# A convolution block with a cubic spline behind it: two products move from VectorE to GpSimd, one add from TensorE to VectorE

## The reference

```python
# layer 0: sign-weight convolutions, batch norm over the whole batch
out = relu(batchnorm(conv3x3(x, sign(w1)), gamma1, beta1))
x = relu(batchnorm(conv3x3(out, sign(w2)), gamma2, beta2) + x)
# layer 1: a cubic B-spline per channel, 32 control values a = mix @ alpha_table
u = (clip(x * a + b, -1.5, 1.5) + 1) * 0.5 * 31
i, t = floor(u), u - floor(u)
spline = sum over n of alpha_table[clip(i - 1 + n)] * basis_n(t)
return id_gain * x + einsum(spline, mix) + bias
```

## Time and profile before

| what | value |
|---|---|
| median of 3 runs | 1145.0 us (1142.17 to 1150.26) |
| the profiled execution, its own time | 1146.37 us |
| its span, first to last instruction | 1144.5 us |
| TensorE busy | 1082.0 us (95%) |
| VectorE busy | 966.5 us (84%) |
| ScalarE busy | 899.1 us (79%) |
| GpSimd busy | 139.3 us (12%) |
| spline part, first sum to end | 418 to 1144.5 us |

### The profile page before, as it was taken

The page is one execution under the profiler, slowest core; times in us unless marked ns, Lnnn a source line. Parts: engine busy times, 40 slices in busy tenths (PEclk is TensorE's granted clock), DMA queues, the critical chain, the costliest instruction groups (busy, mean ns, idle before and its releaser), DMA issues.

```text
span 1144.5 us, 53175 instructions
## 1 busy us (share of the span) xinstructions
PE 1082.0 (95%) x24650; PEld 733.9 (64%) x24650; DVE 966.5 (84%) x959; ACT 899.1 (79%) x410; POOL 139.3 (12%) x195
## 2 busy tenths in 40 slices
PE   6999999699999968999999999999999999999996
PEld 5777777577777745556676565566666566665564
DVE  4855656696767779999999989989999999999997
ACT  4445443666777648999999999989999999999971
POOL 6000000058100000111101101110101101101000
PEclk9999999899999989999999999999999999999998
DMA  8577674677777837799999989989999998999652
GB/s 275 204 291 281 267 281 170 234 243 289 272 273 298 343 167 159 187 234 225 222 222 227 231 200 228 224 207 233 222 223 217 230 233 196 235 220 226 162 133 87
DMA packets 57465, 259.46 MB, mean 227 GB/s; under 512 B 16080, under 2 KB 16080, under 8 KB 49232
## 3 DMA queue, kind: packets, MB, share of 16 engines
q1 hardware_dynamic: 48496, 208.40, 56.5%
q0 software_dynamic: 8640, 48.17, 22.9%
q10 hardware_dynamic: 160, 0.30, 0.1%
HBM read 104.29 MB, written 77.07 MB: 158 GB/s over the span
## 4 chain that ended last, share of the span: by engine, by line
PE 86%; DVE 7%; issue 4%; DMA 1%; ACT 1%; SPq 0%; DVEq 0%; ACTq 0%
PE tab L1302 48%; PE acc L741 30%; PE tab L1312 7%; DVE middle_mask L1160 1%; DMA halo<-y_scratch 1%; DVE far_sq L1209 1%; DMA w_raw<-in_w 1%; ACT xin L381 1%; ACT yout L420 1%; DVE poly L1201 0%; DVE far L1187 0%; DVE stats L547 0%; DVE offset L1153 0%; DVE poly L1215 0%; DVE band_split L509 0%
## 5 line engine op out<-in xcount | busy, mean ns | idle before, releaser
L1302 PE MATMUL tab<-edge_mask,diag 128*32 128x392 bf16 x10240 | 448.1, 329 | 7.5 <-issue 3.9
L1302 PEld LDWEIGHTS tab<-edge_mask,diag 128*32 128x32 f16 x10240 | 287.4, 97 | 159.4 <-issue 20.5
L1057 ACT ACTIVATE edge_mask<-cell,thr 128x6272 bf16<-128x6272 bf16 x62 | 338.6, 5508 | 1.3 <-DMA cell<-cell 1.3
L420 ACT ACTIVATE yout<-acc 128x1568 f32<-128x1568 f32 x64 | 94.5, 1477 | 169.7 <-PE acc L741 149.1
L741 PE MATMUL acc<-split,w 64*64 64x385 f16 (+3 forms) x4608 | 192.6, 327 | 12.4 <-DVE w L468 10.0
L741 PE MATMUL acc<-band_split,w 64*64 64x385 f16 (+3 forms) x4608 | 194.2, 329 | 10.6 <-DVE band_split L509 4.6
L1302 PE MATMUL tab<-middle_mask,diag 128*32 128x392 bf16 x4096 | 189.0, 329 | 11.2 <-issue 8.9
L547 DVE BATCH_NORM_STATS2 stats<-yout 128x392 f32 (+1 forms) x240 | 117.9, 555 | 90.8 <-ACT yout L420 90.8
L741 PEld LDWEIGHTS acc<-band_split,w 64*64 64x64 f16 x4608 | 150.6, 109 | 54.0 <-issue 8.8
L741 PEld LDWEIGHTS acc<-split,w 64*64 64x64 f16 x4608 | 145.6, 108 | 58.7 <-issue 13.6
L1302 PEld LDWEIGHTS tab<-middle_mask,diag 128*32 128x32 f16 x4096 | 112.1, 97 | 76.5 <-issue 13.7
(11 more groups left out here) (140 smaller groups left out, 963.4 us busy)
## 6 DMA issues: line engine op xcount, KB each, us to landing
y_scratch<-yout SPq DMA_DIRECT2D x32, 1568.0 KB, 6.1
cell<-cell SPq DMA_DIRECT2D x496, 98.0 KB, 5.2
xin<-y_scratch SPq DMA_DIRECT2D x16, 1568.0 KB, 6.2
lin<-far POOLq DMA_DIRECT2D x32, 784.0 KB, 9.7
out<-lin SPq DMA_DIRECT2D x31, 784.0 KB, 5.7
xin<-in_x SPq DMA_DIRECT2D x15, 1568.0 KB, 6.7
lin<-y_scratch SPq DMA_DIRECT2D x30, 784.0 KB, 9.4
lin<-in_x POOLq DMA_DIRECT2D x28, 784.0 KB, 8.0
```

Of the source, the lines that this page charges most:

```text
L420: act.activation(yout[b][:, :].rearrange("p (r k x) -> p k r x", r=2, k=TILES)[:, 2 * part:2 * part + 2], acc[:, 4 * part:4 * part + 4, 0: ...
L1057: act.activation(mask_of(c, q)[:, :, :], cell4[c % 2][:, :, :], ACT.Sign, bias=thr[:, q:q + 1]).then_inc(sign_mask_ready, 1)
L1302: mm = pe.matmul(tab[(c + t) % 2][j * GROUP:(j + 1) * GROUP, sub, 0:SUB], keep["diag"][part][:, j % 2, t, q, :], mask_of(c, q)[:, j, sub * ...
```

## The change

The near product is no longer added by TensorE: `add_near_part` is gone, and VectorE's `square` adds the near product (in `poly`) to the square table as it reads it from PSUM. The multiplication by d^2 that `square` did before is a GpSimd `tensor_tensor`, `square_term`, in place on `poly`. Its result goes into `lin` by the accumulating DMA that carried the far part before (`add_square`). The far product is the second GpSimd `tensor_tensor`, `far_part`; it stays in `far`, and VectorE's `slope_and_far` and `value` add slope and value to it there. The slope goes in place over `offset`. To make the plain product do, the amplitude is rounded to a power of four and its root is put into the scale of `distance_square` (`ROOT`).

One block of four of the first edge mask moves from ScalarE to VectorE (`edge_block`, as 0 or 2 instead of -1 or +1). In the last chunk VectorE does both products and the add itself. The near table takes its quads in the order 2, 0, 1, 3.

```diff
-QUADS_OF = (QUAD_ORDER, QUAD_ORDER, EDGE_QUADS, EDGE_QUADS, EDGE_QUADS)
+NEAR_ORDER = (2, 0, 1, 3)
+FAR_ORDER = (2, 3, 0, 1)
+QUADS_OF = (NEAR_ORDER, FAR_ORDER, EDGE_QUADS, EDGE_QUADS, EDGE_QUADS)
...
-            for c in range(CHUNKS):
+            def far_part(c):
+
+                pool.wait_ge(table_used, used(c, T_FAR))
+                pool.wait_ge(far_sq_ready, c + 1)
+                pool.tensor_tensor(far[c % 2][:, :], far[c % 2][:, :], far_sq[:, :],
+                                   ALU.mult).then_inc(far_part_ready, 1)
+
+            def square_term(c):
+
+                pool.wait_ge(table_used, used(c, T_SQ))
+                pool.wait_ge(dist_sq_ready, c + 1)
+                pool.tensor_tensor(poly[c % 2][:, :], poly[c % 2][:, :], dist_sq[:, :],
+                                   ALU.mult).then_inc(square_ready, 1)
+
+            def add_square(c):
+
+                pool.wait_ge(square_ready, c + 1)
+                pool.wait_ge(lin_ready, c + 1)
+                pool.dma_start(lin_of(c)[:, :], poly[c % 2][:, :], accum_op=ALU.add).then_inc(square_added[c % 2], 16)
+
+            for c in range(CHUNKS - 1):
                 if AHEAD <= c + 3 < CHUNKS:
                     add_x(c + 3)
-                add_far(c)
+                far_part(c)
+                square_term(c)
+                add_square(c)
...
-                act.activation(mask_of(c, q)[:, :, :], cell4[c % 2][:, :, :], ACT.Sign,
+                blocks = slice(0, 3 if q == EDGE_QUADS[0] else 4)
+                act.activation(mask_of(c, q)[:, blocks, :], cell4[c % 2][:, blocks, :], ACT.Sign,
                                bias=thr[:, q:q + 1]).then_inc(sign_mask_ready, 1)
...
-                dve.wait_ge(table_ready, used(c - 1, T_FAR))
+                dve.wait_ge(middle_used, c)
...
             def square(c):
 
-                dve.wait_ge(dist_sq_ready, c + 1)
+                dve.wait_ge(table_used, used(c, T_NEAR))
                 dve.wait_ge(table_ready, used(c, T_SQ))
                 dve.scalar_tensor_tensor(out=quarters(poly[c % 2]), in0=summed(c, T_SQ), scalar=base(c, T_SQ),
-                                         in1=quarters(dist_sq), op0=ALU.add,
-                                         op1=ALU.mult).then_inc(table_used, 1)
+                                         in1=quarters(poly[c % 2]), op0=ALU.add,
+                                         op1=ALU.add).then_inc(table_used, 1)
...
+            def slope_and_far(c):
+
+                dve.wait_ge(table_used, used(c, T_LIN))
                 dve.wait_ge(far_part_ready, c + 1)
...
+                dve.scalar_tensor_tensor(out=far[c % 2][:, :], in0=sloped(c), scalar=1 / POINT,
+                                         in1=far[c % 2][:, :], op0=ALU.mult, op1=ALU.add).then_inc(slope_ready, 1)
...
                 dve.wait_ge(table_used, used(c, T_VAL))
-                dve.wait_ge(far_added, 16 * (c + 1))
-                dve.scalar_tensor_tensor(out=lin_of(c)[:, :], in0=poly[c % 2][:, :], scalar=cc(AMP),
+                dve.wait_ge(square_added[c % 2], 16 * (c // 2 + 1))
+                dve.scalar_tensor_tensor(out=lin_of(c)[:, :], in0=far[c % 2][:, :], scalar=cc(AMP),
                                          in1=lin_of(c)[:, :], op0=ALU.mult, op1=ALU.add).then_inc(whole, 1)
...
-                if t == T_SQ:
-                    pe.wait_ge(table_used, used(c, T_NEAR))
-                    for sub in range(4):
-                        mm = add_near_part(c, sub)
+                    if t == T_FAR and q == MIDDLE_QUADS[-1]:
+                        mm.then_inc(middle_used, 1)
```

More of the change, by code:

```diff
@@ L867, in spline @@
         dist_sq_ready = sem("dist_sq_ready")
-        slope_ready = sem("slope_ready")
+        square_ready = sem("square_term_ready")
+        edge_block_ready = sem("edge_block_ready")
+        slope_ready = sem("slope_and_far_ready")
+        square_added = [sem(f"square_term_added{b}") for b in range(2)]
+        last_square_added = sem("last_square_term_added")
+        middle_used = sem("middle_masks_used")
         whole = sem("chunk_whole")
@@ L1208, in slope @@
[L1208 to L1216 removed]
+                dve.wait_ge(dist_ready, c + 1)
@@ L1262, in _ @@
             total(3)
+            offsets(1)
+            middle(1, MIDDLE_QUADS[0])
             far_cube(0)
+            edge_block(1)
             linear(0)
-            far_part(0)
-            middle(1, MIDDLE_QUADS[0])
             square(0)
-            offsets(1)
             slope(0)
-            middle(1, MIDDLE_QUADS[1])
-            add_slope(0)
+            slope_and_far(0)
             value(0)
-            linear(1)
-            linear(2)
             for c in range(1, CHUNKS):
-                if c > 1:
-                    value(c - 1)
+                middle(c, MIDDLE_QUADS[1])
+                if c == 1:
+                    linear(1)
+                    linear(2)
                 if c + 2 < CHUNKS:
@@ L1281, in _ @@
                 near_cube(c)
-                finish(c - 1)
-                far_cube(c)
-                far_part(c)
-                if c + 1 < CHUNKS:
-                    middle(c + 1, MIDDLE_QUADS[0])
-                square(c)
                 if c + 1 < CHUNKS:
                     offsets(c + 1)
+                    middle(c + 1, MIDDLE_QUADS[0])
+                    edge_block(c + 1)
+                far_cube(c)
+                if c == CHUNKS - 1:
+                    last_far_part()
+                square(c)
+                finish(c - 1)
+                if c == CHUNKS - 1:
+                    last_square_term()
                 slope(c)
-                if c + 1 < CHUNKS:
-                    middle(c + 1, MIDDLE_QUADS[1])
-                add_slope(c)
+                slope_and_far(c)
+                if c < CHUNKS - 1:
+                    value(c)
             closing_quarters()
@@ L1297, in _, with product @@
         def _(pe):
-            def product(c, t, q, sub):
+            def product(c, t, q, sub, order=None):
+                order = order or QUADS_OF[t]
                 for part in range(2):
@@ L1304, in product @@
                                        mask_of(c, q)[:, j, sub * SUB:(sub + 1) * SUB],
-                                       start=(q == QUADS_OF[t][0] and part == 0),
-                                       stop=(t != T_SQ and q == QUADS_OF[t][-1] and part == 1))
-                return mm
-            def add_near_part(c, sub):
-                for j in range(4):
-                    mm = pe.matmul(tab[(c + T_SQ) % 2][j * GROUP:(j + 1) * GROUP, sub, 0:SUB],
-                                   keep["ident"][:, j * GROUP:(j + 1) * GROUP],
-                                   poly[c % 2][:, sub * SUB:(sub + 1) * SUB], start=False, stop=True)
+                                       start=(q == order[0] and part == 0),
+                                       stop=(q == order[-1] and part == 1))
                 return mm
@@ L1337, in first_table @@
                         for sub in (2 * h, 2 * h + 1):
-                            mm = product(0, T_NEAR, q, sub)
+                            mm = product(0, T_NEAR, q, sub, QUAD_ORDER)
                 mm.then_inc(table_ready, 1)
```

89 lines of the change are left out of this document (56 added, 33 removed).

## The result

The changed kernel takes 1214.0 us (median of four runs, 1213.4 to 1215.6) against 1146.2 for the kernel before, measured beside it (1142.2 to 1150.3). The ratio is 1.059, with a 95% interval of 1.055 to 1.063: slower by 68 us, where 30 us less was forecast, and 24 us above the end of the range. It went as rival A says, and by more.

The account below looks back on a forecast made before the run. TensorE was taken to bound the kernel at 21.92 us per chunk, other engines and DMA within 7%. 30 x (21.92 - 20.85) = 32.1 us less and 2.9 more at the end gave 1116 us, range 1096 to 1190.

Parts of the forecast that it names:

- rival A: GpSimd products and VectorE passes with two SBUF inputs block each other: 2.7 us more in the loop, 1192 us; chance 0.33.
- the VectorE part of the loop: VectorE passes from `square` to the second middle mask, taken at unheld lengths: 10.85 us of the loop.
- the one-way hold in rows 10 and 12: Old profile: GpSimd's L337 and L349 ended only behind VectorE passes with two SBUF inputs; L349 took 3.32, alone 0.36.
- I put the average at 20.85 rather than 20.3: Average period per chunk, set above the loop's 20.3 us for tight DMA and queue and for TensorE pauses.
- The walk's 20.3: Loop through TensorE's 9.34 us, VectorE's 10.85 and a semaphore's 0.12, claimed to set the period of a chunk.
- the allowance of 0.55: What the forecast average of 20.85 us per chunk adds to the loop's 20.3 for DMA, queue and pauses.
- rival C: DMA engines or SyncE's queue are the floor: chunks of 20.9 to 21.4 us, 1123 to 1132 us; chance 0.09.
- the likeliest case: The forecast itself, far product starts 20.3 to 21 us apart, a span of 1098 to 1132 us; chance 0.43.
- B's second wait: No-change rival, GpSimd holds only while reading: waits of 0.5 and 0.6 us per chunk, 1149 us; chance 0.15.
- The start: Time up to chunk 1's first far product: change taken as 0, between -2 and +3 us.
- The end: Time from the last far product on: 19.4 us against 16.6 before, +2.9, bounded by VectorE.
- the mask block: VectorE's new `edge_block` pass, a quarter of an edge mask taken from ScalarE, taken as 0.55 us.

Follow-up runs that it names:

- e1: Changed kernel with both GpSimd products cut to 32 of 1568 columns, the rest not multiplied; 1175.9 us.
- e2: Changed kernel with `slope` written in place into its PSUM table, so `slope_and_far` has one SBUF input; 1182.0 us.
- e4: Changed kernel with `slope` left in PSUM and `finish` moved ahead of `far_cube`; 1149.4 us.
- e9: Changed kernel with each GpSimd product replaced by three fills of the same tile, which read no tensor; 1172.1 us.
- e5: Changed kernel with 64 unneeded TensorE matmuls of 120 columns ahead of the quad that waits for the late middle mask; 1196.5 us.
- e7: e1 with the load of y issued behind 8 of the 16 cell copies instead of ahead of them; 1133.9 us.
- e8: e4 with the load of y issued behind 8 of the 16 cell copies instead of ahead of them; 1139.4 us.

## Why the prediction was wrong

**The mechanism was rival A's.** The step that failed is in the VectorE part of the loop: "finish 1.76", "`slope_and_far` 1.82". They take 0.88 and 1.47 more beside GpSimd's products, 2.35 of the 2.7 that rival A gives. Its places are right as well: `finish` waits for the far part, `square_term` for `finish`, `slope_and_far` for `square_term`. e1, e2, e4 and e9 show the cause from four sides.

**Why it had only 0.33.** The reading against it was L520, which ran at its normal 3.42 us from 16.89 on, though L336 was on the record until 17.44. One overlap of 0.55 us at a record's end, on an engine whose records are rough, was set against a rule, against the one-way hold in rows 10 and 12 and against the argument that a lock stops both. In the spline part the held pass ends 1.64 or 1.65 us behind GpSimd's record, so the hold lasts to within 0.2 us of its end. Why L520 wasn't held was not tried.

**The size: the clock.** No case had it. With the holds TensorE's pause ahead of the late quad is 2.77 us (1.3 in e1), and the clock fell in two chunks of three. They cost 1.65 and 1.44 us more than the third, 1.03 on average, 31 us in all. e5 takes the clock's fall away and gives 17.5 us back; its own average is still 0.38 above its clean chunks (23.21 against 22.83). Its trace has 14.8 us of TensorE's pauses for nothing shown, which the changed kernel's has not; where they come from is open.

**"I put the average at 20.85 rather than 20.3": too near.** The walk's 20.3 was good: 20.49 in clean chunks of e7, and 22.86 - 2.35 = 20.5 in the changed kernel. But the allowance of 0.55 was too small. Of the two floors named in rival C the queue was a real one, though not for its 14.0 us of issuing: the load in it waits for a store's landing with the copies behind, 22.76 in e1 against 21.28 in e7. Even without holds, clock and queue the average is 21.3 in e7. Its trace has 26.0 us of TensorE's pauses for nothing shown, where the kernel before has 12.6; that these now stand in the loop is likely, not shown. So without a hold the forecast would have been too low by 30 x 0.43 = 13 us for the loop alone, and e7 (which multiplies 2% of the columns) is at 1133.9, just above the 1132 to which the likeliest case reached.

**Two sums of the rivals.** B's second wait doesn't follow from its own walk: `finish` until 4.9, `square_term` from 6.7 to 9.7, `slope_and_far` due at 8.5 make 1.2 and not 0.6, 1.7 in all and about 1167 instead of 1149. C's ends of 20.9 to 21.4 would be 1117 to 1132, not 1123 to 1132. Neither changes the forecast.

**The sum by its terms,** in us: holds 2.35, clock and irregular chunks 1.02, walk 0.2, less the allowance of 0.55, makes 3.02 per chunk, 90.7 in all (23.88 - 20.85 = 3.03). The start cost 5.6 where I took 0. Three rows of VectorE's timeline in the changed kernel:

```profile
445.19 1.85 DVE L1197 TENSOR_SCALAR middle_mask<-cell,thr 128x6272 bf16<-128x6272 bf16 x1 [1.06 <-DMA cell<-cell]
...
449.26 4.30 DVE L1176 TENSOR_SCALAR lin<-lin,cst,par_sb 128x1568 f32<-128x1568 f32 x1
...
457.11 3.48 DVE L1255 SCALAR_TENSOR_TENSOR far<-offset,far 128x1568 f32<-128x1568 f32 x1
```

The mask of chunk 1, ahead of the first far product, waits 1.06 for the copies, and behind that product `linear` and `slope_and_far` of chunk 0 are held, by 3.2 and 1.7. The end, 1189.4 to 1208.7, is 19.3 against 19.4. So 90.7 + 5.6 - 0.1 = 96.2; the profiled executions differ from the forecast for them by 1213.55 - 1117.2 = 96.4.

**What held:** GpSimd's product (3.5; 3.56), the mask block (0.55; 0.62), the length of the loop without holds, the landing of the accumulating DMA in time (no wait of `finish` for it), and the end.

## What to carry to other kernels

Work moved to GpSimd isn't free beside every VectorE pass. Write down for each pass in that window whether it reads two SBUF tensors or is a `tensor_scalar` from SBUF to SBUF (both were held here, passes with a PSUM input were not), and count the hold from whichever engine starts first. Moving one operand to PSUM took the hold away here. A wait of TensorE can cost more than its length: price a loop through it with the clock behind the pause, as a case of its own, since the clock fell behind most pauses of 2.77 us and not behind all. And when the engine that bounds is relieved, the gain goes only down to the next queue, with its waits for landings and not its issue time alone: the matmuls saved are 30 x 2.63 = 79 us, and e8, without holds and without the queue's wait, is 5 us faster than the kernel before.
